# Own places for the 31 output tiles of an expert layer, unpaced row stores, and five routing groups for six

## The reference

```python
x = L0_attn_x
xn = _layernorm(x, axis=-1)
x = x + _L0_attn_ref(xn, ...) + _L0_ffn_ref(xn, routers, W1, W2)
...
# _L0_ffn_ref: L = 4 layers in a row, E = 16 experts, FF = 512
def _unipool_layer(xt, router, W1, W2):
    probs = jax.nn.softmax(xt @ router, axis=-1)
    w, idx = jnp.max(probs, axis=-1), jnp.argmax(probs, axis=-1)
    # the token's expert: silu(xt @ W1[idx]) @ W2[idx], times w
```

## Time and profile before

| | us |
|---|---|
| median of 3 runs | 671.6 (671.29 to 674.56) |
| span of the profiled execution | 669.4 |
| PE busy | 591.2 (88%) |
| DVE busy | 461.0 (69%) |
| ACT busy | 423.6 (63%) |
| POOL busy | 369.0 (55%) |

### The profile page before, as it was taken

The page is one execution under the profiler, slowest core; times in us unless marked ns, Lnnn a source line. Parts: engine busy times, 40 slices in busy tenths (PEclk is TensorE's granted clock), DMA queues, the critical chain, the costliest instruction groups (busy, mean ns, idle before and its releaser), DMA issues.

```text
span 669.4 us, 14542 instructions
## 1 busy us (share of the span) xinstructions
PE 591.2 (88%) x4722; PEld 505.5 (76%) x4722; DVE 461.0 (69%) x1367; ACT 423.6 (63%) x1033; POOL 369.0 (55%) x395
## 2 busy tenths in 40 slices
PE   7879997789988899887999989999896687799996
PEld 7769987749978499885799965796674565668886
DVE  8633455664566655666542078989999999998946
ACT  3365554455555545563466647989988899987442
POOL 5461044540346402454255551278799999998974
PEclk9898998999999799986999989998897789989988
DMA  8953652116421155211443020000000000000002
GB/s 275 335 177 37 175 110 46 37 41 138 100 59 41 34 87 150 58 41 33 63 80 73 32 77 0 2 1 2 1 1 0 1 0 1 1 0 2 3 2 63
DMA packets 104123, 39.86 MB, mean 60 GB/s; under 512 B 85906, under 2 KB 96178, under 8 KB 103922
## 3 DMA queue, kind: packets, MB, share of 16 engines
q1 hardware_dynamic: 98018, 29.34, 19.6%
q0 software_dynamic: 4480, 9.30, 4.1%
q10 hardware_dynamic: 1552, 0.30, 0.2%
HBM read 20.32 MB, written 18.59 MB: 58 GB/s over the span
## 4 chain that ended last, share of the span: by engine, by line
PE 47%; POOL 18%; DVE 14%; issue 8%; ACT 5%; another core or an unknown queue 4%; DMA 2%; SPq 0%; ACTq 0%; POOLq 0%; DVEq 0%
PE PS L2396 18%; PE PS L2381 14%; POOL W1s L894 8%; POOL two_planes L812 4%; DVE W2s L1434 3%; PE PS L2296 2%; POOL wide L816 2%; PE PS L2325 1%; PE PS L2763 1%; PE PS L2287 1%; POOL two_planes L815 1%; ACT wide L1774 1%; PE PS L2780 1%; DMA sorted_x<-xrow,pos 1%
## 5 line engine op out<-in xcount | busy, mean ns | idle before, releaser
L776 POOL DMA_INDIRECT sorted_x<-xrow,pos x93 | 90.3, 971 | 173.0 <-DVE pos L1249 87.3
L2396 PE MATMUL PS<-W2s,wide 128*128 x992 | 146.9, 293 | 22.9 <-ACT wide L1774 12.3
L2396 PEld LDWEIGHTS PS<-W2s,wide 128*128 128x128 f32 x992 | 131.6, 197 | 27.0 <-issue 26.3
L2381 PE MATMUL PS<-wide,swt 128*128 128x128 f32 x992 | 133.6, 279 | 0.9 <-DVE wide L1314 0.9
L2381 PEld LDWEIGHTS PS<-wide,swt 128*128 128x128 f32 x992 | 122.6, 194 | 1.3 <-DVE swt L1308 1.3
L1774 ACT ACTIVATE wide<-PS 128x512 f32<-128x512 f32 x124 | 73.3, 591 | 65.2 <-PE PS L2381 37.6
L1782 ACT ACTIVATE xrow<-PS,tags 128x144 f32<-128x144 f32 (+1 forms) x124 | 46.7, 376 | 58.8 <-PE PS L2396 45.8
L894 POOL TENSOR_TENSOR W1s<-W1s,kT 128x1024 f32<-128x1024 f32 x21 | 50.0, 2385 | 8.2 <-DVE W1s L1581 7.0
L1994 ACT ACTIVATE W1s<-W1s,ab 128x128 f32<-128x128 f32 x168 | 51.4, 401 | 4.5 <-DVE W1s L1581 4.3
L1308 DVE COPY swt<-W1s 128x512 f32 x64 | 27.4, 430 | 37.0 <-PE PS L2381 27.8
L1317 DVE STREAM_TRANSPOSE wide<-wide 128x128 f32<-128x128 f32 x116 | 33.4, 300 | 28.0 <-DMA wide<-sorted_x 27.3
(11 more groups left out here) (434 smaller groups left out, 1320.9 us busy)
## 6 DMA issues: line engine op xcount, KB each, us to landing
wide<-sorted_x SPq DMA_DIRECT2D x224, 32.0 KB
sorted_x<-wide SPq DMA_DIRECT2D x9, 520.0 KB, 3.3
W1s<-in_L_ffn_W_dram SPq DMA_DIRECT2D x1, 4096.0 KB
sorted_x<-wide SPq DMA_DIRECT2D x1, 2015.0 KB, 12.1
sorted_x<-xrow,pos POOLq DMA_INDIRECT x109, 2.8
sorted_x<-wide SPq DMA_DIRECT2D x3, 455.0 KB, 2.9
xres<-in_L_attn_x_dram SPq DMA_DIRECT2D x4, 256.0 KB, 4.8
xrow<-results SPq DMA_DIRECT2D x4, 256.0 KB, 4.1
```

The lines of the kernel that those rows point to most:

```text
L776: pool.indirect_dma_start(xs_dram[l + 1][:, :], bass.IndirectOffsetOnAxis(ap=pos[:, t:t + 1], axis=0), xrow[:, t % NR, 0:XW], None).then_i ...
L2381: m = pe.matmul(PS[:, 2 + n, f * P:(f + 1) * P], w1st[:, (c - 1) % WB, f * P:(f + 1) * P], xring[:, (c - 1) % R, :], start=True, stop=True)
L2396: m = pe.matmul(PS[:, 4 + n, 0:w], hTs[:, n, f * P:(f + 1) * P], W2s[:, f * YW:f * YW + (E - 1) * NF + w][:, bass.ds(w2, w)], start=(f == ...
```

## The change

Each of the 31 tiles of a layer gets its own place in `xrow` (31 slots for 16). With that ACT's wait for a slot's last store goes, and the 16 semaphores of the stores become one. POOL's pacing wait goes: once a group's places are known, its scatters are issued one after the other. The groups become 8, 8, 6, 6 and 3 tiles. `kT`, which isn't needed at the same time, moves into the tail of `xrow`, and two small index tables into a buffer that is free at the start.

```diff
-    GROUPS = ((0, 8), (8, 16), (16, 20), (20, 24), (24, 28), (28, NS))
+    GROUPS = ((0, 8), (8, 16), (16, 22), (22, 28), (28, NS))
...
-    PACE = (10, 9, 8)
-
-
-    CHOOSE_AT = {12: 0, 20: 1, 24: 2, 27: 3}
-    WEIGH_AT = {13: 0, 21: 1, 25: 2, 28: 3}
-    ROOMS_AT = {14: 0, 22: 1, 26: 2, 28: 3}
-    PLACE_AT = {15: 0, 23: 1, 26: 2, 28: 3}
-    TANH_AT = {10: 0, 18: 1, 22: 2, 26: 3, 29: 4}
-    RANKS_AT = {11: 0, 19: 1, 24: 2, 27: 3, 30: 4}
+
+
+    CHOOSE_AT = {12: 0, 20: 1, 26: 2}
+    WEIGH_AT = {13: 0, 21: 1, 27: 2}
+    ROOMS_AT = {14: 0, 22: 1, 28: 2}
+    PLACE_AT = {15: 0, 23: 1, 28: 2}
+    TANH_AT = {10: 0, 18: 1, 24: 2, 29: 3}
+    RANKS_AT = {11: 0, 19: 1, 26: 2, 30: 3}
...
-        xrow = sb("xrow", [P, NT, YW])
-        xcur = xrow[:, :, 0:D]
+        xrow = sb("xrow", [P, NS, YW])
+        xrow_f = xrow[:, :, :].rearrange("p t d -> p (t d)")
+        xcur = xrow[:, 0:NT, 0:D]
...
-        kT = sb("kT", [P, N])
+        kT = xrow_f[:, NS * YW - N:NS * YW]
...
-        y_put = [sem(f"y_put{r}") for r in range(NR)]
+        y_put = sem("y_put")
...
-                    for r in range(NR):
-                        sp.wait_ge(y_put[r], 16 * PUTS[r] * l)
+                    sp.wait_ge(y_put, 16 * NS * l)
...
                     for t in range(*GROUPS[g]):
-                        if g < len(PACE):
-                            pool.wait_ge(y_ev, l * NS + min(NS, t + PACE[g]))
                         pool.indirect_dma_start(xs_dram[l + 1][:, :], bass.IndirectOffsetOnAxis(ap=pos[:, t:t + 1], axis=0),
-                                                xrow[:, t % NR, 0:XW], None).then_inc(y_put[t % NR], 16)
+                                                xrow[:, t, 0:XW], None).then_inc(y_put, 16)
...
                     act.wait_ge(y_mm, at + t + 1)
-                    if t >= NR:
-                        act.wait_ge(y_put[t % NR], put_through(l, t - NR))
                     w = YW if l < L - 1 else D
                     act.wait_ge(tags_ready, 2 * l + (1 if t < R else 2))
-                    act.activation(xrow[:, t % NR, 0:w], PS[:, 4 + c % 2, 0:w], ACT.Copy,
+                    act.activation(xrow[:, t, 0:w], PS[:, 4 + c % 2, 0:w], ACT.Copy,
                                    scale=tags[:, t, 1:2]).then_inc(y_ev, 1)
```

More of the change, by code:

```diff
@@ L158, in build @@
     assert D == P and NT == NR and B == 2 and L == 4 and TB == 2 * HB and GROUPS[-1][0] < NS <= P and N <= TR
+    assert NT * YW + N <= NS * YW
     UNIT_AT = [sum(1 + j1 - j0 for b, h, j1, j0 in UNITS[:n]) for n in range(len(UNITS) + 1)]
@@ L206, in build @@
         after = sb("after", [P, P])
-        row_i = sb("row_i", [P, NS], I32)
-        rev_i = sb("rev_i", [P, E], I32)
         rev = sb("rev", [P, E])
@@ L236, in build @@
         dist_i = hbuf[:, 0:S].bitcast(I32)
+        row_i = hbuf[:, S:S + NS].bitcast(I32)
+        rev_i = hbuf[:, S + NS:S + NS + E].bitcast(I32)
         hTs = hbuf[:, 0:2 * FF].rearrange("p (b f) -> p b f", b=2)
@@ L321, in build @@
         Kc = qT[:, :].rearrange("p (t h i) -> p t h i", t=C, h=HP)
-        Qc = kT[:, :].rearrange("p (t h i) -> p t h i", t=C, h=HP)
+        Qc = kT.rearrange("p (t h i) -> p t h i", t=C, h=HP)
         Vc = vtok[:, :, :].rearrange("p t d -> p (t d)").rearrange("p (t h i) -> p t h i", t=C, h=HP)
         bKc = wdec[:, :, :].rearrange("p b (t h i) -> p (b t) h i", h=HP, i=HD)
-        xcur_f = xrow[:, :, :].rearrange("p t d -> p (t d)")[:, 0:XN]
+        xcur_f = xrow_f[:, 0:XN]
         X = [v.rearrange("p (c h i) -> p c h i", h=HP, i=HD) for v in (xcur_f, u[0][:, 0:XN], u[0][:, XN:2 * XN])]
@@ L350, in build @@
         vT = u[7].rearrange("p (b t) -> p b t", b=B)
-        vsq = kT[:, :].rearrange("p (b t) -> p b t", b=B)
+        vsq = kT.rearrange("p (b t) -> p b t", b=B)
         vstd, vinv = mx, first
@@ L510, in build @@
         SLOT_USES = [[c for c in PAIR_AT if c // 2 % RP == r] for r in range(RP)]
-        PUTS = [(NS - r + NR - 1) // NR for r in range(NR)]
         def pair_loaded(l, c):
@@ L516, in pair_loaded @@
             return 16 * (P // SQ) * (l * len(uses) + uses.index(c - c % 2) + 1)
-        def put_through(l, c):
-            return 16 * (l * PUTS[c % NR] + c // NR + 1)
         def group_slots(g):
@@ L671, in _ @@
                             matrix_part(1)
-            for r in range(NR):
-                sp.wait_ge(y_put[r], 16 * PUTS[r] * L)
+            sp.wait_ge(y_put, 16 * NS * L)
             for g in range(NG):
@@ L708, in _ @@
             step(pool.iota(row_i[:, 0:NT], pattern=[[P, NT]], base=0, channel_multiplier=1))
-            step(pool.tensor_copy(xrow[:, :, D], row_i[:, 0:NT]))
+            step(pool.tensor_copy(xrow[:, 0:NT, D], row_i[:, 0:NT]))
             step(pool.memset(ones_bf[:, :], 1.0))
@@ L781, in _ @@
                 pool.indirect_dma_start(y_dram[:, :], bass.IndirectOffsetOnAxis(ap=pos[:, t:t + 1], axis=0),
-                                        xrow[:, t % NR, 0:D], None).then_inc(y_put[t % NR], 16)
+                                        xrow[:, t, 0:D], None).then_inc(y_put, 16)
             step(pool.memset(ebias, 0.0))
@@ L1162, in choose @@
                 dve.wait_ge(y_ev, l * NS + GROUPS[g][1])
-                lg = xrow[:, tt, D:YW]
+                lg = xrow[:, GROUPS[g][0]:GROUPS[g][1], D:YW]
                 step(dve.tensor_reduce(mx[:, tt], lg, AX_X, ALU.max))
@@ L1186, in weigh @@
                 step(dve.reciprocal(ex[:, tt, :], ex[:, tt, :]))
-                mark(dve.tensor_reduce(xrow[:, tt, D + 1], ex[:, tt, :], AX_X, ALU.add))
-                mark(dve.tensor_copy(xrow[:, tt, D], tags[:, GROUPS[g][0]:GROUPS[g][1], 0]))
+                own = slice(*GROUPS[g])
+                mark(dve.tensor_reduce(xrow[:, own, D + 1], ex[:, tt, :], AX_X, ALU.add))
+                mark(dve.tensor_copy(xrow[:, own, D], tags[:, own, 0]))
             def weigh_last(l):
                 i, tt = NFG + (l + 1) * NGR - 1, group_slots(NGR - 1)
-                mark(dve.tensor_copy(xrow[:, tt, D], tags[:, GROUPS[NGR - 1][0]:NS, 0]))
+                own = slice(*GROUPS[NGR - 1])
+                mark(dve.tensor_copy(xrow[:, own, D], tags[:, own, 0]))
                 dve.wait_ge(exp_done, i + 1)
                 step(dve.tensor_reduce(esum[:, tt], ex[:, tt, :], AX_X, ALU.add))
-                return mark(dve.tensor_scalar(xrow[:, tt, D + 1], esum[:, tt], float(E), 0.5, ALU.add, ALU.mult))
+                return mark(dve.tensor_scalar(xrow[:, own, D + 1], esum[:, tt], float(E), 0.5, ALU.add, ALU.mult))
             def rooms(l, g):
```

## The result

The changed kernel takes 705.7 us (median of 4 runs, 704.66 to 711.89) where the kernel before, run beside it, takes 672.3 (671.29 to 674.56): 1.054 times as long, interval 1.050 to 1.059. The forecast was 697, with a range of 673 to 709. The profiled execution of after has a span of 703.1 us, 33.7 more than before's 669.4, where the prediction's sum said 26.

A forecast was written before the change was run, and what follows sets the result against it. Closely spaced POOL scatters were taken to keep PE's finished products from ACT, stalling the tile loop. Loop and tail terms, 27.2 over three layers less 0.75 and 0.3, gave +26: span 695.5, median 697, range 673 to 709.

The forecast's parts named there:

- the signs given for it: Two eight-scatter runs per layer, 1.5 tiles or so in ten us, ACT idle 6 us or more, 2.6 us more at the tail.
- First group: Tile loop, first eight scatters now issued in a row: 6.6 us lost against 2.4, +4.2 per layer (bounds +3.6 and +5.8).
- The 6.6: Price of a burst of eight, from the first routing's (6.0 to 7.2), other bound 8.2 from extending bursts of five.
- Second group: Tile loop, five in a row then three singly become eight in a row: 6.6 less 4.35, +2.25 per layer (0 to +3.85).
- price of 4.35: Mean loss in before's loop while the second group, with its burst of five, is scattered, without its rank products.
- Third group: Third and fourth groups merged into six: six scatters close together before and after, so 0, with 1 us either way.
- the -0.75 of the rank products: One set of rank products (0.25) fewer per layer from merging groups: 0.75 us gained in three layers.
- Tail: Layer's end, last but one group of six instead of four: two more scatters and held last places, +2.6; 0.9 without stretching hold.
- Sum: (4.2 + 2.25 + 0 + 2.6) x 3 layers = 27.2, less 0.75 and 0.3: +26 us.
- The capped hold: Rival: PE is let through now and then, so eight scatters cost what five do; +10, 682 us, chance 0.17.
- the bursts aren't the cause: Rival: loop unchanged, only the tail's 0.9 and the savings count; +1.7, 673 us, chance 0.11.
- A price per row: Rival "faster": loop price goes by rows scattered, 0.47 each, not by packing; -6.7, 665 us, chance 0.10.

The follow-up runs named there:

- e2: The changed kernel with the pacing wait put back for its first three groups: 673.2 us beside 672.2, ratio 0.9995.
- d1: The kernel before plus extra back-to-back scatters to a spare tensor in a loop's quiet part: two cost 0, four 0.9, eight 7.9 us.
- d3: The kernel before plus eight extra scatters a layer: four pairs with memsets between lose nothing, short memsets between lose 4.5 us, back-to-back 32-byte rows 8.6.
- e4: The changed kernel with a 0.54 to 0.69 us memset between any two scatters of the first three groups: 655.2 us beside 666.3, ratio 0.983.
- e5: The changed kernel with a memset after every second scatter of the first three groups, on another chip: 638.3 us beside 622.4, ratio 1.026.
- e7: The kernel before, unpaced, with a memset after every second scatter of all groups but the last: 640.5 us beside 622.4, ratio 1.030.
- e1: The kernel before with only its pacing wait taken away: 693.7 us beside 672.2, ratio 1.030.
- e8: The changed kernel with a memset after every second scatter of the first three groups, on the fourth chip: 657.8 us, ratio 0.979 to before.

## Why the prediction was right, and where its sum was not

- *Which change costs.* The prediction put own places, one semaphore and the wait that ACT loses at nothing. e2 measured 0.9995. Right.
- *What costs.* Unpaced scatters hold back PE's updates: right, by d1 to d3 and e4, on two chips, and by the repeat on a third, though not on the chip of e5 to e7, which has no such hold. Of the signs given for it, the two runs of eight came as said. But three tiles' products start in the ten us of the first (24 of them from 87.20 to 97.22), not one and a half, and no wait of ACT before a SiLU or an output copy of the three layers is over 4.4 us, where 6 or more were expected: the hold lets an update through in between.
- *First group, +4.2 (6.6 in place of 2.4).* It was +5.7 on average (9.7, 6.1 and 9.7 less some 2.8). The term was under-sized in both its parts. The 6.6 came from the burst in the first routing: 3.45 + 1.06 of standing still, and some 2.1 of products at less than their pace. There PE still had products to do for 8.6 us after the burst began (34.47 to 43.11, when the 3.45 begin), so that only the rest of the hold reached it. In the tile loop PE needs ACT at every tile: in layer 0 it is 0.89 + 5.37 = 6.3 of lateness and 1.91 + 0.92 = 2.8 of products at 1.2 GHz, 9.1, rank products aside. The slow products were in the sum, if not by the name of the clock, at too small a size.
- *Second group, +2.25.* It was +4.4 (27.0 less 13.8, over three). The same error, and before's price of 4.35 holds a clock of 0.86 to 1.00 itself.
- *Third group, 0.* The rest of the loop changed by 29.7 less 30.3, -0.6 in three layers, near the -0.75 of the rank products. Right, and for the reason given: six scatters close together in before, by backlog of its pacing, and six after. e1, which has four and four, loses 4.3 us less there than after.
- *Tail, +2.6 a layer.* It was 0.9, 0.6 and 1.2, on average just under the lower bound of 0.9. The profile of after at the end of layer 0, on POOL, PE and DVE, and the same DVE line in layer 1:

```profile
151.45 0.96 POOL L768 DMA_INDIRECT sorted_x<-xrow,pos  x1 [0.30 <-issue]
153.66 0.97 POOL L768 DMA_INDIRECT sorted_x<-xrow,pos  x1 [1.24 <-issue]
...
149.20 0.42 PE L2263 MATMUL PS<-room,ones_row 1*128 1x48 f32 x2
...
152.25 0.21 DVE L1215 SCALAR_TENSOR_TENSOR selbuf<-PS,shift 128x48 f32<-128x48 f32 x1 [2.04 <-remote]
...
245.06 0.21 DVE L1215 SCALAR_TENSOR_TENSOR selbuf<-PS,shift 128x48 f32<-128x48 f32 x1 [0.26 <-PE PS L2263]
```

  The burst is longer by 2.54, as said, and DVE was indeed held, 2.04 us. But the term let the hold stretch with the burst, so that DVE would again be served 0.9 after its end, and that failed. In before DVE was served 0.93, 0.97 and 0.92 after the burst's last scatter in layers 0 to 2, so the earlier trace rows was no accident; in after it was served 0.16 and 0.15 before that ends in layers 0 and 2, and in the middle of the burst in layer 1, 3.1 before its end. From the burst's start to the last group's it is 8.56, 7.64 and 8.56 in place of 7.11, 7.14 and 7.10. In layer 0 that is 2.54 less 1.09, 1.45.
- *Sum.* +18.6 of loop and +7.8 of tail were forecast, less 0.3; 29.7 and 2.6 were found. Two errors of opposite sign, 11 and 5 us, with the 1.4 elsewhere, leave 8 of the 33.7 unforeseen. The time falls in the range, but the loop carries nearly all of it. That is partly luck: with the tail as forecast it would have been some 711, past the range's 709.
- *The rivals.* The capped hold (682) falls: five cost 4.35, eight 7.9 in d1. Yet what spoke for it is real: one update does get through in mid-burst (ACT at 95.92), and ACT's waits in the first burst are two, of 3.74 and 2.52 us. That the bursts aren't the cause (673) falls with d1. What spoke for it was the rule of the Trainium skill, page "SBUF — State Buffer", section "SBUF: two separate sides", that DMA and compute engines can't slow each other. On three chips ACT and DVE wait beside a burst of scatters; on the chip of e5 to e7 they don't. The rule is about the memory's ports, and the traces don't show whether the memory is where the hold happens, so they don't decide on it. A price per row (665) falls: four cost 0.9, eight 7.9.

Open stay what in the chip keeps the updates back, why one chip of four doesn't, and what the change itself does there, where neither it nor any unpaced burst in a tile loop was run.

## What to carry to other kernels

A wait that looks idle can be what spaces a queue: before taking a pacing wait out, look for "remote" or unknown links in the chain and at what is issued closely beside them. Size such a price from a burst in the same loop, slow products after the stall included, and put pauses only where the issuing engine has time left, since they move to the end of its queue. Measure on more than one chip: a cure for a stall that one chip doesn't have costs its own price there.

## What the runs showed of the hardware

- Scatters of 128 rows from POOL, 1.27 us apart, keep PE's completions from ACT and DVE on three of the four chips of the experiments. In one trace two cost a loop of 1.87 us a tile 0 us, four 0.9 and eight 7.9, of which 1.7 is slower products after 5.8 us idle. Rows of 32 bytes cost as much as rows of 512 (8.6 us beside 7.9).
- A pause of 0.54 us or more after every scatter removes it, after every second it removed it in one place (d3) and left 1.2 to 1.4 us in each of three tiles in another (e8), and 0.17 leaves over half.
- Eight plain stores of the same bytes, 0.57 us each back to back, 4.56 in all, cost nothing.
- The same program takes 622 us on one chip and 666 to 672 on three others at a mean granted clock little apart (0.95 to 0.97 beside 0.92 to 0.95). By stages, an estimate, some 42 of the 50 us lie up to the first output product and in the four loops; no experiment isolates the hold there.
